# Macaron block with a gated delta-rule recurrence on one core: constant waits and per-slot semaphores in the recurrence loop

## The reference

```python
x = x + 0.5 * ffn(layernorm(x))        # Win -> 64 relu nets of 16 -> Wout
x = x + attn(layernorm(x))             # below
x = x + 0.5 * ffn(layernorm(x))
# attn: 16 heads of 32
h = rmsnorm(x, ln1_scale)
q, k, v = h @ wq + bq, h @ wk + bk, h @ wv + bv
k = k / (norm(k) + 1e-6); beta = sigmoid(h @ wbeta + bbeta)
for each token t:                      # Sm: 32 x 32 for each head
    delta = v_t - Sm @ k_t
    Sm = Sm + beta_t * outer(delta, k_t)
    o_t = Sm @ q_t
x = o @ wo + bo + residual
x = gelu(rmsnorm(x, ln2_scale) @ w1 + b1) @ w2 + b2 + x
```

## Time and profile before

| | |
|---|---|
| median of 3 runs | 3310.53 us (3310.06 to 3311.02) |
| span of the profiled execution | 3309.8 us |
| TensorE busy | 3179.2 us, 96% |
| VectorE busy | 1841.6 us, 56% |
| ScalarE busy | 1308.4 us, 40% |
| GpSimd busy | 1205.1 us, 36% |
| recurrence | 971 to 1721 us |

### The profile page before, as it was taken

One profiled execution on the slowest core, in us unless ns is written; L12 is line 12 of the kernel. 1 busy time (PEld: TensorE's weight loads), 2 busy tenths in 40 slices (PEclk: granted clock), 3 DMA queues, 4 the chain that ended last, 5 costly groups with the idle time before them and its releaser, 6 DMA issues.

```text
span 3309.8 us, 150288 instructions
## 1 busy us (share of the span) xinstructions
PE 3179.2 (96%) x68438; PEld 2594.1 (78%) x68438; DVE 1841.6 (56%) x2965; ACT 1308.4 (40%) x2654; POOL 1205.1 (36%) x1211
## 2 busy tenths in 40 slices
PE   5999999999958999999999999999999999999998
PEld 4777777777747888898888778887777888777886
DVE  6787878778648899888323333233333323333324
ACT  5444445444313333333343333333333433333333
POOL 1435564655526776666211222211222212122211
PEclk8999999999969999999999999999999999999999
DMA  3445555455465677666661110101110110111010
GB/s 111 144 148 167 141 162 154 145 152 162 139 201 181 220 227 228 215 197 207 200 184 35 39 39 13 39 26 39 39 39 17 36 39 26 39 39 38 14 39 26
DMA packets 388865, 356.00 MB, mean 108 GB/s; under 512 B 58256, under 2 KB 321680, under 8 KB 385680
## 3 DMA queue, kind: packets, MB, share of 16 engines
q1 hardware_dynamic: 386400, 351.86, 34.2%
q10 hardware_dynamic: 2224, 0.90, 0.2%
HBM read 184.65 MB, written 153.09 MB: 102 GB/s over the span
## 4 chain that ended last, share of the span: by engine, by line
PE 65%; DMA 2%; SPq 0%; DVE 0%; issue 0%; ACT 0%; DVEq 0%; ACTq 0%
PE bank L237 14%; PE bank L235 14%; PE bank L236 14%; PE bank L1238 13%; PE bank L1283 5%; PE bank L1698 2%; PE bank L1689 2%; DMA ringB<-heads_scratch 1%; PE bank L1681 1%; PE bank L1672 1%; DMA Z<-z_scratch 0%; DVE g L2010 0%; PE bank L1745 0%; SPq L1147 0%; ACT relu L1867 0%
## 5 line engine op out<-in xcount | busy, mean ns | idle before, releaser
L1939 DVE TENSOR_TENSOR glo<-gl,gh 128x512 fp32r<-128x512 f32 x256 | 196.0, 766 | 823.5 <-ACT gh L1817 821.8
L1813 ACT ACTIVATE gl<-bank,b1m 128x512 f32<-128x512 f32 x256 | 176.0, 687 | 736.4 <-PE bank L237 730.9
L235 PE MATMUL bank<-h,w_hi 128*128 128x512 f32 x1024 | 421.1, 411 | 0.1
L235 PE MATMUL bank<-w_hi,gh 128*128 128x512 f32 x1024 | 402.7, 393 | 0.9 <-DVE glo L1939 0.9
L237 PE MATMUL bank<-h,w_lo 128*128 128x512 f32 x1024 | 401.3, 392 | 0.0
L237 PE MATMUL bank<-w_hi,glo 128*128 128x512 f32 x1024 | 400.5, 391 | 0.0
L236 PE MATMUL bank<-h,w_hi 128*128 128x512 f32 x1024 | 399.4, 390 | 0.0
L236 PE MATMUL bank<-w_lo,gh 128*128 128x512 f32 x1024 | 399.2, 390 | 0.0
L236 PEld LDWEIGHTS bank<-h,w_hi 128*128 128x128 f32 x1024 | 193.4, 189 | 49.2 <-issue 10.7
L235 PEld LDWEIGHTS bank<-h,w_hi 128*128 128x128 f32 x1024 | 192.5, 188 | 48.7 <-issue 10.8
L1238 PE MATMUL bank<-ringA 32*32 32x32 f32 x16512 | 221.9, 196 | 5.3 <-issue 4.3
(11 more groups left out here) (200 smaller groups left out, 7086.1 us busy)
## 6 DMA issues: line engine op xcount, KB each, us to landing
ringB<-heads_scratch SPq DMA_DIRECT2D x257, 192.0 KB, 3.3
ringA<-heads_scratch SPq DMA_DIRECT2D x260, 128.0 KB, 2.8
X<-in_L_attn_x SPq DMA_DIRECT2D x16, 1024.0 KB, 10.1
x_scratch<-X SPq DMA_DIRECT2D x16, 1024.0 KB, 4.5
heads_scratch<-vb SPq DMA_DIRECT2D x16, 1024.0 KB, 5.2
heads_scratch<-qk SPq DMA_DIRECT2D x16, 1024.0 KB, 6.6
heads_scratch<-kb SPq DMA_DIRECT2D x16, 1024.0 KB, 5.2
heads_scratch<-kbuf SPq DMA_DIRECT2D x16, 1024.0 KB, 7.2
```

Source lines behind the costliest of these rows:

```text
L235: e.matmul(o, lhs[0], rhs[0], start=first, stop=False)
L1813: e.activation(gl[k][:, :], bank[1 - k][:, :], ACT.Gelu_apprx_tanh, bias=b1m[:, m:m + 1]).then_inc(a_gl, 1)
L1939: e.tensor_tensor(gh[k][1][:, :], gl[k][:, :], gh[k][0][:, :], ALU.subtract).then_inc(v_gl, 1)
```

## The change

The matrix engine's waits on a register become waits on a constant, wherever ScalarE or a load releases them. For that, `a_delta`, `a_state` become four semaphores each, one for each ring slot, and a matmul of the body that runs once the wait is passed takes the value off again (`then_inc(sem, -1)`, for loads -16 or -32). Only the waits for VectorE's `v_olo` and `v_z` still compare with a register. Delta and state are split in two halves, `front` and `back` (groups 0, 1 and 2, 3), and the waits for slots and for v_olo and v_z stand between them, or behind the body's last product, and no longer in front of the groups that need them.

For this, slot 3 of ringB is set to zero by Pool as a stand-in for the first turn, and SyncE's first load of it waits for the first `out_delta`. It stands in the queue ahead of the loads of wo and of the first 2 MB system.

On ScalarE, `normalize`, the w1 pieces, the squares and the w2 pieces move behind the copy of sT in chunk 4b+3; the normalization there is that of block b itself. VectorE's rest of a w1 piece moves from chunk 4b+2 to chunk 4b+4, between its two `low` of that block.

```diff
             def load_b(c):
-                if c >= 4:
+                if c >= 3:
                     e.wait_ge(p_o, c - 2)
...
-            def tiles(out, lhsT, rhs, first):
+            def tiles(out, lhsT, rhs, first, groups=range(GROUPS)):
...
             def out_delta(j):
-                tiles(outputs(j), de[j % 2], split(ringB[:, j, RP, :]), False).then_inc(p_o, 1)
+                made = tiles(outputs(j), de[j % 2], split(ringB[:, j, RP, :]), False)
+                made[0].then_inc(a_state[j], -1)
+                made[-1].then_inc(p_o, 1)
...
+                    e.wait_ge(a_state[0], 1)
+                    delta(0, front)[0].then_inc(d_A[1], -32)
+                    delta(0, back)[-1].then_inc(p_delta, 1)
+                    values(2)
+                    keys(2)
+                    e.wait_ge(a_delta[0], 1)
+                    state(0, front)[0].then_inc(d_A[2], -32)
+                    state(0, back)[-1].then_inc(p_state, 1)
+                    out_state(3)
+                    out_delta(3)
+
+                    e.wait_ge(a_state[1], 1)
+                    made = delta(1, front)
+                    made[0].then_inc(a_delta[3], -1)
+                    made[1].then_inc(d_B[3], -16)
+                    e.wait_ge(d_B[1], 16)
+                    delta(1, back)[-1].then_inc(p_delta, 1)
+                    values(3)
+                    keys(3)
+                    e.wait_ge(a_delta[1], 1)
+                    state(1, front)[0].then_inc(d_A[3], -32)
+                    e.wait_ge(v_olo, out)
+                    e.reg_add(out, out, 4)
+                    state(1, back)[-1].then_inc(p_state, 1)
+                    out_state(0)
+                    out_delta(0)
...
+                    e.wait_ge(a_state[3], 1)
+                    delta(3, front)
+                    e.wait_ge(d_B[3], 16)
+                    e.wait_ge(v_olo, out)
+                    e.reg_add(out, out, 0)
+                    delta(3, back)[-1].then_inc(p_delta, 1)
...
+                    e.wait_ge(a_delta[3], 1)
+                    state(3, front)
+                    e.wait_ge(v_z, out)
+                    e.reg_add(out, out, 4)
+                    state(3, back)[-1].then_inc(p_state, 1)
+                    out_product(range(12))
+                    e.wait_ge(d_A[2], 32)
+                    e.wait_ge(d_A[3], 32)
+                    e.wait_ge(d_B[0], 16)
...
-                if at == 0 and blk:
-                    normalize(blk - 1)
+                if at == 3 and blk + 1 < NBLK:
+                    normalize(blk)
                 i = piece2(blk)
-                if at == 1 and i is not None:
+                if at == 3 and i is not None:
...
                     if s >= 2:
-                        for j in range(4):
-                            e.wait_ge(d_A[j], 32 * (NC // 4) * s)
+                        e.wait_ge(p_R, NC * s)
...
-                i = piece2(blk)
-                if at == 2 and i is not None:
+                i = piece2(blk - 1)
+                if at == 0 and i is not None:
                     e.wait_ge(a_w1hi, i + 1)
...
             e.memset(sT[0][:, :, :], 0.0).then_inc(o_s0, 1)
+            e.memset(sT[3][:, :, :], 0.0).then_inc(a_state[3], 1)
+            e.memset(de[1][:, :, :], 0.0).then_inc(a_delta[3], 1)
+            e.memset(ringB[:, 3, :, :], 0.0).then_inc(d_B[3], 16)
```

More of the change, by code:

```diff
@@ L1223, in pe_delta @@
         def pe_delta(e):
-            def tiles(out, lhsT, rhs, first):
-                for n in range(GROUPS):
+            def tiles(out, lhsT, rhs, first, groups=range(GROUPS)):
+                made = []
+                for n in groups:
                     for h in range(4):
                         r = slice(32 * h, 32 * h + 32)
-                        m = e.matmul(out[r, n, :], lhsT[r, n, :], rhs[r, n, :], start=first and n == 0, stop=True,
-                                     skip_group_check=True)
-                return m
+                        made.append(e.matmul(out[r, n, :], lhsT[r, n, :], rhs[r, n, :], start=first and n == 0,
+                                             stop=True, skip_group_check=True))
+                return made
             def split(b):
@@ L1285, in out_product @@
                         m.then_inc(p_wo, 1)
+            front, back = range(0, 2), range(2, GROUPS)
             e.wait_ge(done1, 5)
-            e.wait_ge(o_s0, 3)
+            e.wait_ge(o_s0, 1)
             e.matmul(bank[B_STATE][:, 0:P], heads(sT[0][:, :, :]), heads(sT[0][:, :, :]), start=True, stop=True)
-            for j in range(2):
-                e.wait_ge(d_A[j], 32)
-                ahead(j)
+            e.wait_ge(d_A[0], 32)
+            values(0)
+            keys(0)
+            e.wait_ge(d_A[1], 32)
+            values(1)[0].then_inc(d_A[0], -32)
+            keys(1)
             e.wait_ge(d_A[2], 32)
@@ L1298, in pe_delta @@
             e.wait_ge(d_B[3], 16)
-            with e.register("now") as now, e.register("out") as out, e.register("slot_a") as slot_a, \
-                    e.register("next_a") as next_a, e.register("slot_b") as slot_b, e.register("next_b") as next_b:
-                e.reg_mov(now, 1)
+            e.wait_ge(a_state[3], 1)
+            e.wait_ge(a_delta[3], 1)
+            with e.register("out") as out:
                 e.reg_mov(out, 4)
-                e.reg_mov(slot_a, 64)
-                e.reg_mov(next_a, 64)
-                e.reg_mov(slot_b, 16)
-                e.reg_mov(next_b, 32)
@@ new lines, in pe_delta @@
+                    state(1, back)[-1].then_inc(p_state, 1)
+                    out_state(0)
+                    out_delta(0)
+                    e.wait_ge(a_state[2], 1)
+                    made = delta(2, front)
+                    made[0].then_inc(a_delta[0], -1)
+                    made[1].then_inc(d_B[0], -16)
+                    e.wait_ge(d_B[2], 16)
+                    e.wait_ge(d_A[0], 32)
+                    delta(2, back)[-1].then_inc(p_delta, 1)
+                    out_state(1)
@@ new lines, in pe_delta @@
+                    out_delta(1)
+                    made = keys(0)
+                    made[0].then_inc(a_delta[1], -1)
+                    made[1].then_inc(d_B[1], -16)
+                    e.wait_ge(a_delta[2], 1)
+                    state(2, front)
+                    e.wait_ge(d_A[1], 32)
+                    state(2, back)[-1].then_inc(p_state, 1)
+                    values(0)
+                    values(1)[0].then_inc(d_A[0], -32)
+                    e.wait_ge(a_state[3], 1)
+                    delta(3, front)
```

89 lines of the change are left out of this document (23 added, 66 removed).

## The result

Ten runs of the changed kernel gave a median of 3319.97 us (3313.78 to 3322.77), ten of the kernel before on the same chip 3311.14 us (3310.06 to 3314.61): a ratio of 1.0025, 95% interval 1.0016 to 1.0035. The change makes the kernel slower by a quarter of a per cent. Forecast were 3300 us and, with the highest chance, a gain. The profiled execution has a span of 3320.3 us, against 3309.8.

A forecast was written before the change was run, and what follows sets the result against it. The prediction took the recurrence's chain of matrix-engine matmuls and ScalarE copies as the bound. Terms -32 + 10 + 6 + 4 + 2 = -10 took the profiled span from 3309.8 to 3299.8, so 3300 us; range 3266 to 3320.

The forecast's parts named there:

- together a body loses 0.68 us, to 10.34: Recurrence: an ordinary body, eight steps of deltas and states totalling 11.02 us, loses 0.68; 47 bodies give -32 us.
- Constant waits: Five latency steps of a body: load follows ScalarE's copy by 0.05 us, not 0.09; 0.22 us saved a body.
- The inner gaps of steps 5 and 7: Two steps with four matmul groups ahead of the state: 1.33 to 1.15 and 1.25 to 1.13, 0.30 us saved.
- three register waits coming back: Between halves of a delta or state: about 0.07 us each, 0.2 us a body, only if the queue had not run ahead.
- Step 8: The body's last step, 3.35 us: the output product with changes of shape at its ends; no saving claimed there.
- The normalization, 0.16 us: ScalarE: moved to the body's end, it no longer delays the copy of delta(1); 0.16 us saved a body.
- step 3: From delta(1) to state(1), 1.15 us: taken as a latency loop of small matmuls and a ScalarE copy, delayed by the normalization.
- (a): VectorE: w1_lo ahead of the second oT_lo in odd bodies delays delta(3)'s middle by 0.83 us in 12 bodies, +10 us.
- (b): Body pairs around a 2 MB load: the normalization waits for z's store, holding the next body's first copy; five pairs, +6 us.
- (c): Start: ringB slot 3's load waits for the first out_delta, delaying the first system load; VectorE's lag stays, +4 us.
- (d): RingB slot 3, needed earlier, in delta(3): late landings cost +2 us; body 53 swaps Z0's square for slot 3, 0.
- the constant wait is worth nothing: Rival for the recurrence: only the normalization's 7.5 us is won against 22 of costs, 3325 us; chance 0.10.

The follow-up runs named there:

- e2_dec_off: The changed kernel with five decrements moved from the waiting matmul to the next one; 3313.2 us, ratio 1.0004 to the kernel before.
- r2_nomov_only: The changed kernel without the addition of 0 behind the wait for v_olo in delta(3); 3315.71 us, ratio 1.0009 to the kernel before.
- g4_nomov: The changed kernel with decrements off waiting matmuls, 2 MB load in uneven pieces, b1 and b2 loads behind the last z store, no addition of 0; 3299.55 us.
- e4_act_only: The kernel before with only ScalarE's and VectorE's part of the change; 3323.93 us, ratio 1.0040 to the kernel before.
- r1_rec_only: The kernel before with only the recurrence's part of the change, ScalarE's and VectorE's orders as before; 3316.24 us, ratio 1.0012.
- e8_more_events: The changed kernel with four more always fulfilled waits per body, on matmuls of the second output products; 3323.66 us, ratio 1.0035 to the kernel before.
- e3_sys_late: The changed kernel with the 2 MB load later in SyncE's queue, before the block's last ringA load; 3317.86 us, ratio 1.0019 to the kernel before.
- e1_norm_back: The changed kernel with the normalization back behind the first state copy of the next body; 3321.86 us, ratio 1.0033 to the kernel before.

## Why the prediction was wrong

**The step that failed is "together a body loses 0.68 us, to 10.34".** It came out at 0.12, and carried -5.4 us in place of -32. Its three parts:

*Constant waits, 0.045 us off each of five steps.* The measured operation, 0.05 us from copy to load, is real: after, delta(3) has it. But it is had only where the waiting matmul carries no decrement. Where it also takes a semaphore down, the wait is a separate instruction, and the load starts 0.11 us behind the copy, 0.02 worse than the register wait. I had counted the decrements only as a cost of their own, among the rivals. I took the row from stage 1 for the same form. Its matmul waits and adds to a semaphore (`p_wout`), and TensorE's queue holds no instruction for its wait (none from 36.5 to 37.4 us); what it lacks is a decrement. e2_dec_off shows the gain come when they are moved: 0.1 us a body, 7 us in all.

As a cost of their own the decrements of a body, sixteen of them, are not to be seen: e2_dec_off has as many decrements as the changed kernel, and a body in it is shorter than before by 0.24 us. No run takes them out alone.

*The inner gaps of steps 5 and 7, 0.30 us.* Step 5 gave 0.10 of 0.18. Step 7 grew by 0.04: the waits between the halves put a register move in it, which costs 0.1 us in every body (r2_nomov_only, g4_nomov). I had named three register waits coming back, 0.2 us a body, as what happens if the queue has not run ahead, and took that it has. It has at the output product (1208.8 against 1211); in delta(3) the move starts at 1208.8, 0.2 us behind the delta's first load, and this one operation cost 0.1 us, half of those 0.2. The 0.07 us for each of the three was my estimate and has no row. Step 8 grew by 0.05, which was not foreseen: state(3)'s 32 loads take 0.47 us after and 0.37 before. In body 47 most of that lies in the first sixteen, which start over 0.20 us and not 0.13. All kernels with the new recurrence have that. Loads that follow a stop start closer together than loads in an unbroken flow: in the earlier trace rows the 32 at 1200.42, behind a stop of 0.35 us, start over 0.23 us (0.34 less one load's length), 7.4 ns apart, and the 64 at 1200.67 over 0.58, 9.2 ns apart. Whether step 8 grew by that I haven't isolated. (The prediction's 1.13 us for step 7, where its own four groups want 1.15, and the 0.36 in its upper bound have no row; the first moves the sum by 1 us.)

*The normalization, 0.16 us.* Worth nothing in ordinary bodies (e4_act_only): step 3 ends with the queue's 64 loads of chunk 3, about when the late copy ends. "Step 3 is the same loop as step 1" was the error. In body 47 the group of chunk 3 starts 0.28 us behind the delta's first load, its starts take 0.75 (0.85 less one load's length), and the register wait follows: 1.03 of the step's 1.16 us were queue. I had counted such a group only in steps 5 and 7. Only in the last bodies (54 to 62), where ScalarE had more in front of the copy, does the move show among the bodies counted at 0.68: they fell by 1.7 us, and by 1.5 in e4_act_only.

**(a) w1_lo in odd bodies, +10: some 1.4.** List of waits of bodies 6 to 52 of the changed kernel, us in total, times, longest:

```profile
PE bank L1240 <- DVE oT_lo L1512: 1.9, 5, 0.4
```

Four of the five waits stand where they were forecast, in the middle of delta(3), but in bodies 7, 15, 23 and 31 only. There the second oT_lo ends 6.6 to 6.7 us into the body, near the forecast 6.78, and the body takes 11.3 to 11.4 us; with VectorE's order as before (r1_rec_only) it takes 11.0. In the other odd bodies with a piece it ends at 5.7 to 6.1, in time. The w1_lo that comes into the odd body has left the even one ahead of it, and VectorE enters the odd body with less arrears. These 1.4 us are inside the -5.4 above.

**(b) The pairs, +6: +13.8.** The mechanism and its time were right: the copy was forecast for 1136.4 and came at 1136.61. The size was not. Forecast were state(0) at 1136.7, delta(1) at 1137.7 and state(1) at 1138.6, with 0.4 us won back later. Measured were 1136.98, 1138.02 and 1139.30 and nothing won back, since the body had become hardly shorter. And the stop slows what follows: after 3.17 us without a weight load the granted clock was 0.60, and the two steps took 1.04 and 1.28 us where body 18 needs 1.00 and 1.05; the next took 1.28 where body 18 needs 0.98. In e2_dec_off the first and third of these stops are 2.9 and 3.0 us from load to load, and behind both the clock stayed at 1.00; the first:

```profile
1134.32 0.34 PEld L1240 LDWEIGHTS bank<-de,ringB 32*32 32x32 f32 x32 [2.81 <-ACT de L1403]
```

```profile
1133.50:1136.40 2.90, 2.08 (x213) 2.08 (x217) 0.87 (x2) 1.93 (x7) 2.14 (x3) 1.00 0.79 258
1136.40:1140.00 3.60, 3.60 (x372) 3.53 (x367) 3.46 (x7) 1.28 (x5) 3.21 (x6) 1.00 0.80 208
```

Those two pairs take 24.4 us each. The other three have stops of 3.3 to 3.7 us and take 25.6 to 26.0: 0.3 to 0.7 us more in the stop, 1.2 to 1.7 in the pair. The difference, some 0.9 us a pair, I put down to the clock. e8_more_events bears that out with two stops of the same length, 2.82 and 2.84 us from load to load. What follows them:

```profile
1228.60:1235.40 6.80, 6.79 (x529) 6.77 (x530) 5.22 (x10) 2.30 (x10) 6.09 (x11) 0.57 0.60 180
...
1320.90:1327.70 6.80, 6.79 (x672) 6.77 (x672) 5.40 (x10) 2.75 (x12) 6.17 (x10) 1.00 0.73 211
```

The first pair takes 26.0 us and the second 24.6: with the clock down, 1.4 us more. So the length of a stop alone does not decide whether it falls: in e3_sys_late it was 0.62 over the 3 us behind a stop of 2.52 us.

**(c) The start, +4: -0.3.** Issue and transposes came at 976.24 and 985.44, forecast 975 and 986, and the loop began at 969.38 in place of 971.29. The lag did come, as body 0 took 3.7 us more. The stall on cold code that the prediction puts ahead of p_o goes by these traces with the first pass over the loop's code: before, TensorE's matmuls stand still for 4.66 us in front of 977.90, in the middle of state(0), and body 0 has six such stops of 1.5 to 4.7 us, where body 18, the same code, has none above 0.35; after, the stop in state(0) is 0.96 us. But "the lag stays" was wrong: bodies 1 to 5 took 61.0 us and not 63.0. The normalization's place does it. With it late (e4_act_only) they take 61.1, with it early 62.9 (e1_norm_back, the changed kernel but for this) and 63.7 (r1_rec_only). Before, the matrix engine waits 6.1 us for oT_lo in them, after the change and in e4_act_only 3.8. How the normalization's place brings oT_lo sooner isn't shown.

**(d) Slot 3 late, +2, and body 53, 0.** In ordinary bodies nothing. In body 53 the exchange came as forecast: before, a wait of 3.2 us for ScalarE's copy, held by Z0's square; after, one of 5.3 us in the middle of delta(3) for slot 3, whose load waits behind b2's broadcast, 4.36 us on SyncE. The body took 1.3 us more; since two profiles of the same order differ by 1.4 us there, this term is uncertain.

Sum of what was measured: -5.4 + 13.8 - 0.3 + 1.3 + 1.0 (behind the last body) = 10.4 of the spans' 10.5 us. The rival that came nearest is "the constant wait is worth nothing", 3325, with its sign right; its reasons were not these. The range, 3266 to 3320, just holds the median, by luck: five of the ten runs lie above it.

What stays open: what lengthens step 8 and, in e2_dec_off, steps 4 and 5; why the normalization's place shortens bodies 1 to 5; and what decides whether the clock falls behind a stop.

## What to carry to other kernels

Ask of every step which of two things ends it last, the awaited result or the engine's own queue; a removed latency is worth only the difference (in body 47 of e4_act_only a copy 0.15 us sooner gave 0.01). A wait for a late transfer should stand as late as its data are used: moved half a step ahead, it takes the work between out of hiding (1.1 us a pair by the timeline of r1_rec_only). And put a semaphore's decrement on a matmul that doesn't wait (0.1 us a body in e2_dec_off), and a large load in pieces that no small urgent store has to queue behind; these two edits and one register operation less turned a loss of 9 us into a gain of 16, of which the kernel before could have had some 6 by the pieces alone.

## What the hardware showed unexpectedly

A matmul that both waited and took a semaphore down got its wait as a separate instruction of 51 ns: 0.11 us from the copy's end to the load, against 0.05 when it only waited, and 0.09 to 0.10 with a register wait. In stage 1 a matmul that waited and added to a semaphore had 0.05. Another separate wait cost 0.012 us where nothing was awaited. A register move in the flow of delta(3) cost 0.1 us. TensorE's granted clock was 0.60 over the 3 us behind a stop of 3.17 us, and stayed at 1.00 behind one of 2.81 us; but behind two stops of the same length (2.82 and 2.84 us from load to load, e8_more_events) it was 0.57 and 1.00 over 6.8 us.
